# Channel 0 taken off the other channels, expert bias in row 0 of the products, Fourier sum on ScalarE and GpSimd

## The reference

```
x = x + deformable 3x3 convolution of LN_channels(x)          # layer 0, offsets from a 3x3 convolution
t = tokens(x);  t = t + top-2 of 8 experts of LN(t)           # logits = LN(t) @ router_w + router_b
                                                             # sum over 2 experts of p * (LN(t) @ expert_w[e] + expert_b[e])
x = x + real(ifft2(mix of fft2(LN_channels(x))))              # layer 1, alphas and betas
t = tokens(x);  t = t + 64 experts, each over its top 8 tokens of an image (GELU in between)
```

## Time and profile before

| what | value |
|---|---|
| profiled execution, span | 3877.71 us, 3875.7 us |
| median of the three timed runs | 3873.46 us |
| phase A | about 7 to 1990 us of the span |
| phase BC | about 1998 to 3570 us |
| busy TensorE, VectorE, ScalarE, GpSimd | 3679.2, 2944.7, 1570.9, 1474.4 us |
| granted TensorE clock, mean | 0.956 |

### The profile page before, as it was taken

One profiled execution on the slowest core, in us unless ns is written; L12 is line 12 of the kernel. 1 busy time (PEld: TensorE's weight loads), 2 busy tenths in 40 slices (PEclk: granted clock), 3 DMA queues, 4 the chain that ended last, 5 costly groups with the idle time before them and its releaser, 6 DMA issues. The chain is left out here.

```text
span 3875.7 us, 89814 instructions
## 1 busy us (share of the span) xinstructions
PE 3679.2 (95%) x31511; PEld 2470.7 (64%) x31511; DVE 2944.7 (76%) x9687; ACT 1570.9 (41%) x4565; POOL 1474.4 (38%) x2661
## 2 busy tenths in 40 slices
PE   6999999999999999999979999999999999996667
PEld 5777777777777777777745666666666666654444
DVE  4666666666666666666648999999999999996633
ACT  3444444444444444444411444434343443434224
POOL 4444444444454444444412333333333333333210
PEclk7999999999999999999979999999999999997755
DMA  5655555555555555555527777777777777884789
GB/s 109 108 95 108 100 95 97 96 108 104 91 99 95 108 103 94 96 97 97 88 81 265 270 275 274 272 268 273 277 271 275 267 276 273 285 303 158 268 312 393
DMA packets 611250, 709.81 MB, mean 183 GB/s; under 512 B 62208, under 2 KB 493824, under 8 KB 594416
## 3 DMA queue, kind: packets, MB, share of 16 engines
q1 hardware_dynamic: 505328, 630.10, 58.3%
q10 hardware_dynamic: 104448, 71.85, 6.0%
q0 software_dynamic: 1024, 2.10, 0.2%
HBM read 521.26 MB, written 181.50 MB: 181 GB/s over the span
## 5 line engine op out<-in xcount | busy, mean ns | idle before, releaser
L423 PE MATMUL a_sb<-a_sr,wcv 128*128 128x512 f32 (+3 forms) x2820 | 1052.2, 515 | 0.8 <-DVE a_xo L551 0.8
L405 PEld LDWEIGHTS a_sb<-a_tt,a_win 32*128 32x128 f32 x19008 | 647.0, 186 | 116.3 <-issue 115.5
L423 PEld LDWEIGHTS a_sb<-a_sr,wcv 128*128 128x128 f32 x2820 | 493.1, 190 | 333.9 <-issue 289.1
L405 PE MATMUL a_sb<-a_tt,a_win 32*128 32x144 f32 x19008 | 679.8, 295 | 17.5 <-ACT a_yr L464 11.0
L1171 DVE TENSOR_TENSOR b_P<-b_P,b_x 128x1024 f32<-128x1024 f32 x512 | 620.1, 1212 | 0.0
L509 DVE COPY a_sr<-a_sb 128x432 f32<-128x432 f32 (+14 forms) x1172 | 419.6, 413 | 204.1 <-PE a_sb L405 204.0
L482 ACT COPY a_sr<-a_sb 128x432 f32<-128x432 f32 (+14 forms) x1172 | 362.9, 389 | 356.4 <-PE a_sb L405 356.4
L1074 PE MATMUL b_z<-b_P,b_ew 128*128 128x512 f32 x1024 | 463.4, 596 | 0.0
L1077 PE MATMUL b_z<-b_P,b_ew 128*128 128x512 f32 x1024 | 460.3, 592 | 0.0
L1300 POOL TENSOR_TENSOR b_ss<-b_st 128x12 f32<-128x12 f32 (+2 forms) x139 | 29.9, 215 | 1050.6 <-DVE b_pp L1245 963.5
L545 DVE STREAM_TRANSPOSE a_tt<-a_sx 128x576 f32<-128x576 f32 x520 | 398.7, 768 | 14.2 <-POOL a_sx L576 5.4
(11 more groups left out here) (186 smaller groups left out, 5374.3 us busy)
## 6 DMA issues: line engine op xcount, KB each, us to landing
b_P<-pd SPq DMA_DIRECT2D x128, 2048.0 KB, 7.8
a_win<-xtp SPq DMA_DIRECT2D x2144, 36.0 KB
a_xin<-in_x SPq DMA_DIRECT2D x128, 256.0 KB, 6.0
xtp<-a_tn ACTq DMA_DIRECT2D x128, 256.0 KB, 2.3
x1d<-a_xo SPq DMA_DIRECT2D x128, 256.0 KB, 5.7
b_x<-x1d SPq DMA_DIRECT2D x128, 256.0 KB, 7.7
x2d<-b_xa SPq DMA_DIRECT2D x128, 256.0 KB, 3.5
pw<-x3d SPq DMA_DIRECT2D x128, 256.0 KB, 6.6
```

The lines of the kernel that those rows point to most:

```text
L405: t = e.matmul(d[:, 0:3 * m_, :, NU_ * i:NU_ * i + NU_], win[32 * q:32 * q + 32, half_of(Q, j) % NWH, NWIN // 3 * h + i, :], m, start=(j = ...
L423: t = e.matmul(ob[:, r:r + m, :], k["wcv"][:, 3 * (2 - kr) + kx, :], rows[:, :, t_, :], start=(t_ == 0 and r == 0), stop=(t_ == 8))
```

## The change

- Setup: VectorE takes column 0 of each tap of the convolution's weights off columns 1 to 127 (one instruction). Phase A: two DMAs per group ("load0") spread the input's channel 0 over partitions 16 to 127 and 1 to 15 of `xz`; GpSimd subtracts `xz` from the input ("level"), before VectorE's residual. So x1d holds channel 0, and in the other rows the difference to it. The rarely run `far_rows` does the same.
- "read": the identity's first column is zero and a 137th column brings out channel 0, which goes to `lr` (8 buffers of 9 columns). Once x1 is read, a DMA sets its row 0 to ones ("level", SyncE).
- P's row 0 gets p instead of p/std; `ew`'s row 0 holds the expert biases, less 1 in column 0. The ninth matmul, `pb` and "spread_b" are gone; the spread is three DMAs of 1, 112 and 15 rows.
- `xa`: four ScalarE instructions with channel 0 as bias instead of one copy.
- "x3": ScalarE scales (4 instructions), GpSimd adds (one instruction, 128x512, after "scales" in its order), VectorE's statistics ("stats3"), the store and all that follows come one step later.
- At phase BC's start SyncE waits for `centred`, loads the biases, and only then x1.

```diff
+            elif o[0] == "level":                                  # phase A, GpSimd
+                w.wait_ge(x0_in[G % 2], 32 * (G // 2 + 1))
+                w.wait_ge(convolved, 2 * G + 2)
+                e.tensor_tensor(xin[:, G % NX, :], xin[:, G % NX, :], xz[:, G % 2, :], ALU.subtract
+                                ).then_inc(levelled, 1)
...
-                w.wait_ge(pb_in[G % NPC], 16 * (G // NPC + 1))
-                e.matmul(ZE[u][:, :, :], ebm[:, :], pb[:, G % NPC, :], start=False, stop=True).then_inc(mixed, 1)
...
-                e.copy(xa[:, G % 3], T2[:, :, :]).then_inc(xa_ready, 1)
+                for r in range(4):
+                    t = e.activation(xa[:, G % 3, r, :], T2[:, r, :], ACT.Identity, bias=lr[:, G % NLR, r, 8:9])
+            elif stage == "x3":                                    # ScalarE
+                for r in range(4):
+                    t = e.activation(x3t[:, G % 3, r, :], ZC[:, r, :], ACT.Copy, scale=rsr[:, G, 3 - r:4 - r])
+                t.then_inc(x3_scaled, 1)
...
-                for r in range(4):                                 # VectorE
-                    t = e.scalar_tensor_tensor(out=x3t[:, G % 3, r, :], in0=ZC[:, r, :],
-                                               scalar=rsr[:, G, 3 - r:4 - r], in1=x2r[:, G % 3, r, :],
-                                               op0=ALU.mult, op1=ALU.add)
...
+            elif stage == "x3":                                    # GpSimd
+                w.wait_ge(x2_in[G % 3], 16 * moves(G))
+                w.wait_ge(x3_scaled, G + 1)
+                e.tensor_tensor(x3t[:, G % 3], x3t[:, G % 3], x2r[:, G % 3], ALU.add).then_inc(x3_ready, 1)
...
     def sync(e):
+        w.wait_ge(centred, 5)
+        e.dma_start(ew[0:1, :, :], ins["eb"][:, :, :]).then_inc(eb_in, 16)
...
+                for c, n in ((16, 112), (1, 15)):
+                    e.dma_start(P[c:c + n, G % NPB].rearrange("p r e x -> p (r e x)"),
+                                pd[G % NPT * 64 + 32:G % NPT * 64 + 64, :]...partition_broadcast(n)
```

More of the change, by code:

```diff
@@ L48, in setup_phase @@
     sem = lambda n: ctx.enter_context(nc.semaphore("s_" + n))
-    filled, loaded, w_in, summed, centred = (
-        sem(n) for n in ("filled", "loaded", "w_in", "summed", "centred"))
+    filled, loaded, w_in, summed, centred, wcv_in = (
+        sem(n) for n in ("filled", "loaded", "w_in", "summed", "centred", "wcv_in"))
     T = ctx.enter_context(nc.psum_tensor("s_t", [128, 162], F32))
@@ L62, in _ @@
                                    op0=ALU.mult, op1=ALU.add).then_inc(centred, 1)
-            e.wait_ge(centred, 1)
+            e.wait_ge(wcv_in, 16)
+            e.tensor_tensor(k["wcv"][:, :, 1:128], k["wcv"][:, :, 1:128],
+                            k["wcv"][:, :, 0:1].to_broadcast([128, 9, 127]), ALU.subtract).then_inc(centred, 1)
+            e.wait_ge(centred, 2)
         @block.tensor
@@ L284, in phase_a @@
         sem(n) for n in ("rs_step", "z_step", "oc_ready", "hats_ready", "weighed_pool"))
+    levelled = sem("levelled")
     x_in = [sem(f"x_in{i}") for i in range(NX)]
+    x0_in = [sem(f"x0_in{i}") for i in range(2)]
     tn_out = [sem(f"tn_out{i}") for i in range(NTN)]
@@ L900 @@
 NU = 10
[L901 to L907, removed]
+NX1, NPB, NPT, NLR = 9, 3, 4, 8
+STEP = (("load", -3), ("load2", LAG - 2), ("read", 0), ("level", 1), ("turn2", 6), ("fourier", LAG), ("turn3", LAG + 3),
+        ("store2", 6), ("turn_p", 2), ("experts", 4), ("p_out", 2), ("scales", 1), ("best", LAG + 4), ("mixed", 5),
+        ("stats1", 0), ("stats2", 6), ("stats3", LAG + 1), ("x3", LAG), ("store3", LAG + 1), ("spread", 2),
+        ("norm3", LAG + 2), ("gate", LAG + 3), ("experts2", 4), ("place", 5), ("sums", LAG + 4), ("weights", 1),
+        ("turn_scale", 7), ("collect", LAG + 5))
+NS = NG + LAG + 1
 NCH, EC, NW, AHEAD = 8, 8, 8, 3
@@ L938, in order_b @@
     out = [("load", G) for G in range(3)]
-    for s in range(NG + LAG + 5):
+    for s in range(NG + LAG + 6):
         for stage, lag in STEP:
@@ L1048, in tensor @@
         w.wait_ge(centred, 5)
+        w.wait_ge(weights_ready, 2)
         for o in order:
@@ L1059, in tensor @@
                 for r in range(4):
-                    t = e.matmul(RD[:, r // 2, r % 2, 0:136], x1[:, G % NX1, r, :], iw[:, :], start=True, stop=True)
+                    t = e.matmul(RD[:, r // 2, r % 2, 0:137], x1[:, G % NX1, r, :], iw[:, :], start=True, stop=True)
                 t.then_inc(read, 1)
@@ L1076, in tensor @@
                 for x in range(4, 8):
-                    e.matmul(ZE[u][:, :, :], ew[:, x, :], P[:, G % NPB, :, x, :], start=False, stop=False)
-                w.wait_ge(pb_in[G % NPC], 16 * (G // NPC + 1))
-                e.matmul(ZE[u][:, :, :], ebm[:, :], pb[:, G % NPC, :], start=False, stop=True).then_inc(mixed, 1)
+                    t = e.matmul(ZE[u][:, :, :], ew[:, x, :], P[:, G % NPB, :, x, :], start=False, stop=(x == 7))
+                t.then_inc(mixed, 1)
             elif stage == "turn2":
@@ L1187, in vector @@
         w.wait_ge(r_step, 1)
+        e.memset(iw[0:1, 128:136], 0.0).then_inc(weights_ready, 1)
+        w.wait_ge(eb_in, 16)
+        e.tensor_scalar(ew[0:1, :, 0:1], ew[0:1, :, 0:1], -1.0, None, ALU.add).then_inc(weights_ready, 1)
         for stage, G in order:
```

130 lines of the change are left out of this document (77 added, 53 removed).

## The result

| | before | after |
|---|---|---|
| median of the timed runs, us | 3872.43 (4 runs) | 4196.89 (4 runs) |
| profiled execution, span, us | 3877.71, 3875.7 | 4197.18, 4195.3 |
| ratio | | 1.0838 (95%: 1.0819 to 1.0857) |
| one full step of phase BC, us | 11.79 | 14.17 |

The account below looks back on a forecast made before the run. It took VectorE as phase BC's bound, 0.4 us ahead of a loop through GpSimd. Profiled 3877.7 + 50 (steps) + 4.5 (start) + 6 (end) + 0.6 (setup) + 2 (phase A) = 3941, less 4.3: 3937 us, range 3836 to 3956.

Parts of the forecast that it names:

- DMAs: Phase BC: three spreads and the row of ones instead of two issues cost zero, between 0 and 2 us in all.
- A spread that lands late: Rival: P's 15 rows fall to one DMA engine, steps of 21 us, some 1100 us more; chance 0.02.
- The block: Phase BC: GpSimd's addition holds VectorE's two-operand instructions at L1202 for 0.85 us per step, between 0 and 1.05.
- start: Phase BC's beginning: x1's load, issued behind `centred` and the biases, delays the first read by 4.5 us (4.3 to 8.2).
- end: Phase BC's drain: one step more and a longer chain in some ten drain steps, +6 us (3.9 to 12).
- setup: Before phase A: VectorE's subtraction of 1143 columns behind the weights' load, +0.6 us, under 1.3.
- phase A: GpSimd's 1.05 us subtraction fits its idle gap between L576 and L623; with the extra DMAs +2 us (0 to 6).
- The floor of the loop: Phase BC: the loop from `pp` through GpSimd's scales and VectorE's weights back to `pp` takes at least 11.37 us per step.
- Weights: Phase BC, VectorE's stage from L1202 to the end of `pp`: forecast to grow from 6.9 to 7.7 us.
- No block: Rival: VectorE isn't held by GpSimd's addition, steps take 11.37 us, 3838 us in all; chance 0.20.
- the half-hidden block: Rival: GpSimd's addition gets in at VectorE's top-eight instructions, holding it 0.3 to 0.5 us per step, 3877 to 3893 us; chance 0.16.
- TensorE as the bound: Rival: without GpSimd's chain in the way, TensorE's 10.8 us would set phase BC's step, 3769 us; chance 0.02.

Follow-up runs that it names:

- one spread: The kernel after, with P spread by one DMA of 128 rows and no separate row 0 from p: 3963.88 us, ratio 1.0225.
- the chain shortened: The kernel after with P in one DMA, p then copied over row 0, VectorE adding x3, GpSimd's power cut in three, the logits' part first: 3816.96 us.

## Why the prediction was wrong, point by point

**The step that failed** is "*DMAs:* ... Zero, between 0 and 2 us in all." It counted issues and bytes and asked whether P would come in time at the old rate. It never asked whether the rate stays, and it didn't: a spread cut into 1 + 112 + 15 rows has slower packets than one of 128. Measured: packets of 995 ns instead of 669, 2.2 us more per step and +284 us in the kernel before with this alone, and 233 us of the 324 lost in the kernel after. The share of 0.79 was taken as room, but a packet time 1.5 times as long takes 5.35 x 0.49 = 2.6 us more per step from every DMA engine (and the 2 KB packets 1.2). That makes 9.3 + 3.8 = 13.1 us, more than the whole forecast step of 12.2; measured are 0.92 x 14.17 = 13.0.

**The rival "A spread that lands late"** had the right place, a chance of 0.02 and the wrong mechanism: it put the 15 rows on one engine, for steps of 21 us and 1100 us in all. The step is 14.17, and the pair 16 + 112, without a piece of 15 rows, costs 263 us too. Between 0 and 1100 no value was weighed.

**The block** was right in kind and too small in size: 0.85 taken, 1.07 to 1.08 measured, just outside its upper bound of 1.05. The addition takes 1.27 us, not the 1.18 x 512 / 576 of the earlier trace rows, and what L1202 would have used comes off. With 1.07 in the place of 0.85 the sum is 3937 + 117 x 0.22 = 3963 us, and the kernel with one spread took 3963.88. That they meet within 1 us is luck in part: on the chip of that run the kernel before took 3877.7, so the difference is 86 us and not the sum's 89 (3963 - 3873.5). Its steps hold 117 x (12.46 - 11.79) = 79 of the 86, which leaves 8 for the terms of start, end, setup and phase A, put at 13. The 1.05 us that the prediction priced beside its 0.85, with +74 us for the steps, was nearer.

**The floor of the loop,** 11.37 us, held: 11.39 in two kernels. From `pp` to the power's end it is 4.43 us (forecast 4.4). "Weights" took 9.72 in the kernel after (forecast 7.7), with the wait for P in it, and 7.99 with one spread.

**No block** and **the half-hidden block** are refuted by L1253's 1.24 to 1.26 us in all 118 steps in which it starts beside the addition. **TensorE as the bound** is refuted by its 2.74 us of waiting for `pp`, also without the late spread: from 2400 to 3200, 96.2 us in 64 times with one spread, 1.5 each. With the chain shortened (11.25 us per step) VectorE sets the step.

**The small terms.** Setup was forecast at +0.6: the subtraction takes 1.35 us, and phase A's first load went out at 9.33 us instead of 7.48, 1.85 later. Phase BC began 3.0 us later in all, so phase A itself cost about 1.1 (forecast 2); GpSimd's subtraction stands in its gap, though a little longer than 1.05:

```profile
566.44 1.27 POOL L597 TENSOR_TENSOR a_xin<-a_xin,a_xz 128x512 f32<-128x512 f32 x1 [1.67 <-DMA a_xz<-in_x]
```

The first read came at 2010.74 instead of 2005.32, 5.4 later, of which 2.4 belong to the start (forecast 4.5; from the load's issue at 2007.92 to the read it is 2.8 us, under the 3.8 taken as the least):

```profile
2010.74 2.17 PE L1095 MATMUL b_rd<-b_iw,b_x 128*128 128x137 f32 x8 [5.11 <-DMA b_x<-x1d]
```

The end took 13.0 us more (forecast 6, bounds 3.9 to 12). From the 128th group's L1253 to the last top-eight of phase BC it is 93.7 us where it was 79.2, and 83.2 with one spread (77.6 and 78.3 in the two kernels whose spreads cost nothing, so this is good to 2 us). So the term itself is about 4, and the late spread adds about 10, with P waited for up to the last groups:

```profile
3826.34 4.63 DVE L1219 TENSOR_TENSOR b_P<-b_P,b_x 128x1024 f32<-128x1024 f32 x4 [6.74 <-DMA b_P<-pd]
```

The granted clock was left at 1.00. It was 0.94 and 0.96 in the two stretches of the kernel after, and 1.00 from 2400 to 3000 with one spread. TensorE waits for `pp` in both kernels, so neither sum rests on it; what the lower clock cost, no run parts.

## What to carry to other kernels

When a DMA to all 128 partitions is cut, cut its columns or take every second row. Contiguous pieces of rows made the mean packet here 1.4 to 1.8 times as long, and with the DMA engines at 0.79 this outweighed everything else in the change. Price an edit to a transfer by its packets' time, not only by its bytes and issues. To keep one row different, write all 128 and then that row over them: 16 KB and one wait cost no time that the step shows here (11.39 us, the loop's floor).

## What the runs showed of the hardware

- Median time of a 16 KB packet of the spread: 618 ns to 128 rows in one DMA, 625 in even and odd rows, 953 for rows 16 to 127 alone, 959 in 1 + 112 + 15, 989 in 16 + 112, 1285 in rows 0-63 and 64-127. All are of the kernel before with that spread.
- Other traffic suffers too: in the same kernel 2 KB packets took 96 ns in the mean beside 128 rows in one DMA, 209 beside 1 + 112 + 15, 124 beside 16 + 112 and also beside the 112 rows alone, and 130 beside rows 0-63 and 64-127. Why the first split is so much worse is open; the kernel after, which has it too, shows 229.
- A VectorE instruction of 0.17 us with two operands in SBUF took 1.25 beside GpSimd's addition of 128x512, and 0.19 beside a `memset` of the same size. Beside GpSimd's powers of four columns, which read SBUF too, it took 0.18 to 0.19.
